# Attention over 1,601 keys in one core: the last key taken off, the half tile in two passes, other places for the side jobs

## The chip, the cores and the metric

One Trainium2 chip (trn2), one core of it. The metric is the device time of one execution in microseconds. Inputs lie in HBM, laid out beforehand on the host; the time covers one launch.

## The reference

`x` is 16 batches of 256 tokens of width 128, `ctx` 16 batches of 1,601 keys of width 96. All is float32.

```
def xattn(x, context, Wq, Wk, Wv, Wo, bo):        # 16 heads of 64
    q, k, v = (x @ Wq), (context @ Wk), (context @ Wv)
    attn = softmax(q k^T / 8)
    return (attn v) @ Wo + bo
x = x + xattn(layernorm(x), ctx, ...)
x = x + ffn(layernorm(x))     # 32 experts of 64, 4 of them per token by a grouped
                              # choice (2 of 4 groups), and one shared expert of 128
```

## The kernel before, in words

**Products.** Wq Wk^T and Wv Wo are multiplied head by head at the start (`A`, 128x96, and `B_all`, 96x128). A query is then a vector of width 96 that is multiplied with the raw keys, and the attention's output is a mean of raw keys, of width 96, that `B_all` projects. Every operand of a large matmul is split into a rounded part (`_hi`) and the rest (`_lo`), and a product takes three passes: hi x hi, hi x lo, lo x hi.

**Groups.** 16 batches x 4 groups of 4 heads are 64 groups. A group is 1,024 query columns (4 heads x 256 tokens) against 13 tiles of keys: 12 of 128, the last (s = 12) of 65 rows. The group's place in its batch is i (0 to 3).

**Per tile.** `scores(s)` (called qk here; L529, L532, L535) makes 128 x 1,024 scores in one half of the PSUM tile `st`: 3 passes x 2 matmuls of 512 columns. ScalarE takes the exponential twice, into `p_full` (L796) and rounded into `p_hi` (L799). VectorE (L1049; for tiles 3, 5, 7, 9 GpSimd, L410) makes `p_lo`. `weigh(s)` (called pv; L543, L546, L549) adds 3 passes x 2 matmuls to the output in PSUM, `op`, which ScalarE copies out once a group (`oT`, L771, `keep_output`).

**The order on TensorE** in a group is written out: for t = 2 to 12: qk(t), side jobs, pv(t-2), side jobs; then pv(11), scores(0) of the next group, pv(12), scores(1) of the next group. qk(2) of a group waits for the exponentials of its tile 0, pv(0) for the `oT` of the group before and for `p_lo` of tile 0.

**Side jobs** are small pieces of work for other groups, each with one letter. They use the two banks of the PSUM tile `side` in turn: job j waits until job j-2 is drained, that is read by VectorE (`s_drain`, which VectorE raises job by job, in order). `PLACES` and `EXTRA` say which jobs stand before and behind pv in each step t:

```
PLACES = {2: ("MM", "M"), 3: ("MM", "M"), 4: ("MM", "MM"), 5: ("MM", "M"), 6: ("MM", "MM"),
          7: ("MM", "MM"), 8: ("MM", "MY"), 9: ("MM", "MM"), 10: ("MM", "MM"), 11: ("YY", "YT"),
          12: ("", "QQ")}
EXTRA = {2: {5: "L", 6: "N"}, 3: {5: "R"}}
```

- M (32 a group, L475): plain scores of the next group for an upper bound of each query's maximum; VectorE reduces them (L1061), then `combine_max` (L920).
- T (L479): turns the maxima into a row; VectorE copies it (`m_row`, L925) and a DMA on SP's queue (L281) puts it under `qT_hi`, so that the scores come out with the maximum subtracted. scores(0) of the next group waits for it (`s_ml`).
- Y (4 a group, L555): `project_head`, the output of one head of the group before; on VectorE `add_head`: a reciprocal of the denominator (L930), a wait for it, two multiply-adds into `x1` (L933).
- Q (2 a group, L468 to L470): queries of the group after the next; ScalarE keeps hi (L734), VectorE lo (L916).
- L, N (L442), R: tokens of other batches turned, and the router's logits.

At the end of each group VectorE has small steps (`after_jobs`): i = 0 statistics, i = 1 normalisation and expert groups, i = 2 routing weights, i = 3 router scores. GpSimd also splits the next batch's keys, a quarter per group. At the start it splits the whole first batch (L365 to L369), and only then SP starts the loads of the second batch (`load_context`, L276, L277), and behind them the DMA of the first row of maxima.

The last 330 us are the experts (17 steps for each of 8 chunks of 512 tokens); the change leaves them as they are, but for the last group's Y jobs, which stand there.

Of the kernel before, what the change touches and what calls it, by code (L numbers as in the profile page):

```python
# [11 lines left out]
P = 128  # L12
# [6 lines left out]
def xattn_moe(nc, x, ctx_keys, ctx_turned, attn_w, bo, router_wT, router_b, moe_w, out):  # L19
# [6 lines left out]
    NC = 1601  # L26
# [14 lines left out]
    MAXW = KEYS // 4  # L41
    NM = 4 * (GQ // P)
    NCH = T // 4
    YW = D + 1
    OW = DC + 1

    stack = ExitStack()
    with stack:
# [24 lines left out]
        recip = sb(stack, "recip", [P, 2])  # L73
        spare = sb(stack, "spare", [P, 1])
# [38 lines left out]
        p_lo = sb(att, "p_lo", [P, 4, GQ], F32R)  # L113
# [4 lines left out]
        with ExitStack() as landing:  # L118
# [25 lines left out]
        s_set = sem("output_preset")  # L144
# [19 lines left out]
        s_drain = sem("side_job_used")  # L164
        s_sh = sem("context_piece_hi_kept")
# [4 lines left out]
        s_qk = sem("scores_made")  # L170
        s_ex = sem("probabilities_made")
# [89 lines left out]
        def _(sp):  # L261
# [7 lines left out]
            sp.dma_start(B_all[DC:OW, 0, 0:D], bo).then_inc(s_bo, 16)  # L269
# [932 lines left out]
```

## Time and profile before

| | |
|---|---|
| median of 3 runs | 3302.25 us (3302.05 to 3302.41) |
| the profiled execution's own time | 3302.1 us |
| its span, first to last instruction | 3300.3 us |
| TensorE busy | 3269.1 us (99%) |
| VectorE, ScalarE, GpSimd busy | 2383.1, 1938.2, 1069.6 us |
| chain that ended last | TensorE 98% |
| one group in the middle, from one qk(12) to the next | 1500.98 to 1546.41: 45.43 us |

In a timeline a row merges equal instructions in a row; its second figure is the time to the modelled end of the last of them. The first of each pair of matmuls overlaps the end of the one before, so what a piece of work costs TensorE is read as the distance from its start to the start of what follows it, not from its duration.

### The profile page before, as it was taken

What the parts mean: (1) busy time and instruction counts of PE and PEld (TensorE: products, weight loads), DVE (VectorE), ACT (ScalarE), POOL (GpSimd) and SP (SyncE); (2) the same over time, 40 slices, a digit from 0 to 9 for tenths busy, and PEclk for the clock granted to TensorE, in tenths of its full rate; (3) what the DMA queues carried; (4) which work ended last, traced back from release to release, by engine and by line L of the source; (5) the groups of instructions that cost most, each with busy time, mean ns of one, the idle gap of its engine ahead of it and who ended that gap; (6) DMA issues with size and microseconds to landing.
All of it is one profiled execution on the core that took longest, in us unless ns stands there. A gap on an engine that the chain in (4) does not pass through costs nothing.

```text
span 3300.3 us, 40940 instructions
## 1 busy us (share of the span) xinstructions
PE 3269.1 (99%) x15518; PEld 2606.8 (79%) x15518; DVE 2383.1 (72%) x4915; ACT 1938.2 (59%) x2236; POOL 1069.6 (32%) x710
## 2 busy tenths in 40 slices
PE   8999999999999999999999999999999999999999
PEld 6777777777787777877777777777777877777887
DVE  6777777777777777777777777777777777777655
ACT  4565555655556555665556655566655666575554
POOL 4322233222332233322233222322223322225555
PEclk9999999999999999999999999999999999999999
DMA  2000000000000000000000000000000001000000
GB/s 79 1 16 1 16 1 11 6 1 16 1 16 1 16 1 16 1 1 16 1 16 1 16 1 16 1 9 8 1 16 1 16 1 39 1 3 4 7 7 10
DMA packets 8055, 32.39 MB, mean 10 GB/s; under 512 B 1585, under 2 KB 2354, under 8 KB 7474
## 3 DMA queue, kind: packets, MB, share of 16 engines
q1 hardware_dynamic: 7858, 29.78, 2.9%
q8 instruction: 122, 2.00, 0.3%
q14 instruction: 75, 0.61, 0.1%
HBM read 27.41 MB, written 2.10 MB: 9 GB/s over the span
## 4 chain that ended last, share of the span: by engine, by line
PE 98%; DVE 1%; issue 0%; ACT 0%; DMA 0%; POOL 0%; POOLq 0%; DVEq 0%; ACTq 0%
PE st L529 12%; PE st L532 12%; PE st L535 12%; PE op L543 12%; PE op L549 12%; PE op L546 12%; PE side L475 11%; PE side L555 3%; PE st L636 2%; PE st L638 2%; PE st L637 2%; PE side L468 1%; PE side L470 1%; PE side L469 1%; PE op L636 1%; PE op L637 1%
## 5 line engine op out<-in xcount | busy, mean ns | idle before, releaser
L796 ACT ACTIVATE p_full<-st 128x1024 f32<-128x1024 f32 (+1 forms) x832 | 853.8, 1026 | 1128.5 <-PE st L535 1128.4
L1061 DVE TENSOR_REDUCE m_part<-side 128x1 f32<-128x402 f32 x2016 | 1078.2, 571 | 550.6 <-PE side L475 550.6
L410 POOL TENSOR_TENSOR p_lo<-p_full,p_hi 128x1024 fp32r<-128x1024 f32 x256 | 669.2, 2614 | 2063.7 <-ACT p_hi L799 2063.7
L799 ACT ACTIVATE p_hi<-st 128x1024 fp32r<-128x1024 f32 (+1 forms) x832 | 848.6, 1020 | 0.0
L1049 DVE TENSOR_TENSOR p_lo<-p_full,p_hi 128x1024 fp32r<-128x1024 f32 (+1 forms) x576 | 700.3, 1216 | 132.7 <-ACT p_hi L799 132.7
L475 PE MATMUL side<-cT_hi,qT_hi 96*128 96x402 f32 x2016 | 555.2, 346 | 0.0
L529 PE MATMUL st<-qT_hi,cT_hi 97*128 97x512 f32 (+1 forms) x1664 | 538.4, 405 | 2.3 <-DMA qT_hi<-m_row 2.3
L543 PE MATMUL op<-p_hi,v_hi 128*97 128x512 f32 (+1 forms) x1664 | 527.1, 398 | 0.5 <-DVE p_lo L1049 0.5
L532 PE MATMUL st<-qT_lo,cT_hi 96*128 96x512 f32 (+1 forms) x1664 | 524.8, 397 | 0.0
L535 PE MATMUL st<-qT_hi,cT_lo 96*128 96x512 f32 (+1 forms) x1664 | 521.9, 395 | 0.0
L549 PE MATMUL op<-p_hi,v_lo 128*97 128x512 f32 (+1 forms) x1664 | 521.1, 394 | 0.0
L546 PE MATMUL op<-p_lo,v_hi 128*97 128x512 f32 (+1 forms) x1664 | 520.8, 394 | 0.0
L475 PEld LDWEIGHTS side<-cT_hi,qT_hi 96*128 96x128 f32 x2016 | 379.6, 188 | 111.8
L532 PEld LDWEIGHTS st<-qT_lo,cT_hi 96*128 96x128 f32 (+1 forms) x1664 | 308.9, 186 | 79.8
L535 PEld LDWEIGHTS st<-qT_hi,cT_lo 96*128 96x128 f32 (+1 forms) x1664 | 306.8, 184 | 80.8
L549 PEld LDWEIGHTS op<-p_hi,v_lo 128*97 128x97 f32 (+1 forms) x1664 | 270.3, 162 | 115.4
L546 PEld LDWEIGHTS op<-p_lo,v_hi 128*97 128x97 f32 (+1 forms) x1664 | 270.1, 162 | 114.6
L529 PEld LDWEIGHTS st<-qT_hi,cT_hi 97*128 97x128 f32 (+1 forms) x1664 | 296.9, 186 | 32.4 <-issue 2.5
L543 PEld LDWEIGHTS op<-p_hi,v_hi 128*97 128x97 f32 (+1 forms) x1664 | 266.3, 164 | 31.7 <-DVE p_lo L1049 1.4
L427 POOL TENSOR_TENSOR h_lo<-hid,h_hi 128x512 fp32r<-128x512 f32 x136 | 175.9, 1293 | 152.0 <-ACT h_hi L840 151.9
L1128 DVE TENSOR_TENSOR gu_mul<-st,act_g 128x512 f32<-128x512 f32 x128 | 88.5, 691 | 106.6 <-PE side L694 99.0
L933 DVE SCALAR_TENSOR_TENSOR x<-side,recip,x 128x128 f32<-128x128 f32 x512 | 156.1, 347 | 9.0
(164 smaller groups left out, 2606.0 us busy)
## 6 DMA issues: line engine op xcount, KB each, us to landing
keys_nat<-in_ctx_keys SPq DMA_DIRECT2D x16, 624.0 KB, 5.8
keys_tur<-in_ctx_turned SPq DMA_DIRECT2D x16, 603.0 KB, 4.9
gud_raw<-in_moe_w SPq DMA_DIRECT2D x2, 1152.0 KB, 7.8
out_x<-x SPq DMA_DIRECT2D x8, 256.0 KB, 2.0
x<-in_x SPq DMA_DIRECT2D x1, 1920.0 KB, 12.1
qT_hi<-m_row SPq DMA_DIRECT2D x64, 4.0 KB
aw<-in_attn_w SPq DMA_DIRECT2D x2, 448.0 KB, 5.3
aw<-in_attn_w SPq DMA_DIRECT2D x1, 896.0 KB, 9.3
```

Of the source, the lines that this page charges most:

```text
L410: pool.tensor_tensor(p_lo[:, slot(s), :], p_full[:, s % 2, :], p_hi[:, slot(s), :].bitcast(F32), ALU.subtract).then_inc(s_lo_pool, 1)
L475: return pe.matmul(where[:, 0:MAXW], qT_hi[slot][0:DC, tile * P:(tile + 1) * P], cT_hi[par][0:DC, part * MAXW:(part + 1) * MAXW], start=Tr ...
L529: pe.matmul(st[0:m, s % 2, j, :], cT_hi[par][:, keys], qT_hi[slot][:, halves[j]], start=True, stop=False)
L532: pe.matmul(st[0:m, s % 2, j, :], cT_hi[par][0:DC, keys], qT_lo[slot][:, halves[j]], start=False, stop=False)
L535: mm = pe.matmul(st[0:m, s % 2, j, :], cT_lo[par][:, keys], qT_hi[slot][0:DC, halves[j]], start=False, stop=True)
L543: pe.matmul(op[0:OW, j, :], v_hi[par][0:m, s, :], p_hi[0:m, slot(s), halves[j]], start=(s == 0), stop=False)
L546: pe.matmul(op[0:OW, j, :], v_hi[par][0:m, s, :], p_lo[0:m, slot(s), halves[j]], start=False, stop=False)
L549: mm = pe.matmul(op[0:OW, j, :], v_lo[par][0:m, s, :], p_hi[0:m, slot(s), halves[j]], start=False, stop=(s == S - 1))
L796: act.activation(p_full[0:m, s % 2, :], both(st[0:m, s % 2]), ACT.Exp, scale=SCALE)
L799: act.activation(p_hi[0:m, slot(s), :], both(st[0:m, s % 2]), ACT.Exp, scale=SCALE).then_inc(s_ex, 1)
L1049: dve.tensor_tensor(p_lo[0:m, slot(s), :], p_full[0:m, s % 2, :], p_hi[0:m, slot(s), :].bitcast(F32), ALU.subtract).then_inc(s_lo, 1)
L1061: dve.tensor_reduce(m_part[:, at:at + 1], where[:, 0:MAXW], AX.X, ALU.max).then_inc(s_drain, 1)
```

## The change

- The key 1,600 is subtracted from all other keys of its batch (scores and weighted mean change by a constant): GpSimd does it in `shift`, for the first batch whole and for the others a quarter per group behind tile 3. The last key has then score 0 for every query; its exponential e^(-max) comes from `keep_last` on ScalarE (8 columns) and is added to the denominator in `add_head`, by one more VectorE instruction and wait. The key's own contribution to the output and the bias come back by one side job U per batch (i = 1, t = 5): a matmul of 128 columns and one addition on VectorE.
- The tile s = 12 has 64 keys. 128 rows of `cT_hi` hold 64 keys' hi and the same keys' lo, so qk(12) is 2 passes instead of 3; its two halves have to be added: ScalarE copies the lower 64 rows out of `st` (`low_half`), VectorE adds them (`sum_half`), and the exponentials read the sum. `p_hi` and `p_lo` lie one above the other in 128 rows, so pv(12) is 2 passes as well (`weigh_half`).
- M jobs have 400 columns instead of 402.
- Side jobs: QQ of t = 12 stands before pv(10), not behind it; N goes from t = 6 to t = 3.
- scores(1) of the next group stands before pv(12), not behind it; scores(0) waits for `sum_half` instead of for the exponentials.

The diff, cut to its core:

```diff
-                  12: ("", "QQ")}
-        EXTRA = {2: {5: "L", 6: "N"}, 3: {5: "R"}}
+                  12: ("QQ", "")}
+        EXTRA = {1: {5: "U"}, 2: {5: "L", 3: "N"}, 3: {5: "R"}}
...
+            def shift(cols, tiles):
+                n = tiles.stop - tiles.start
+                pool.tensor_scalar(keys_tur[:, cols], keys_tur[:, cols], keys_tur[:, NC:KEYS], None, ALU.subtract)
+                return pool.tensor_tensor(keys_nat[:, tiles, :], keys_nat[:, tiles, :],
+                                          keys_nat[:, S:S + 1, :].to_broadcast([P, n, DC]), ALU.subtract)
...
+            shift(slice(0, NC), slice(0, S)).then_inc(s_ss, 1)
+            pool.wait_ge(s_ss, 1)
+            pool.tensor_copy(v_hi[0][:, :, 0:DC], keys_nat[:, 0:S, :]).then_inc(s_sh, 1)
             pool.wait_ge(s_sh, 1)
+            split_lo(0, slice(0, NC), slice(0, S)).then_inc(s_v, NGB)
...
+            def taken_off(where, batch):
+                pe.matmul(where[:, 0:D], last_T[:, batch:batch + 1].to_broadcast([OW, P]), B_sum[:, :],
+                          start=True, stop=True).then_inc(s_fill, 1)
...
                 for j in range(2):
+                    mm = pe.matmul(st[:, s % 2, j, :], cT_hi[par][0:DC, keys], qT_lo[slot][:, halves[j]],
+                                   start=False, stop=(s == FULL))
+                for j in range(2 if s < FULL else 0):
+                    mm = pe.matmul(st[:, s % 2, j, :], cT_lo[par][:, keys], qT_hi[slot][0:DC, halves[j]],
+                                   start=False, stop=True)
...
-                pe.wait_ge(s_ex, n + S)
+                pe.wait_ge(s_sum, g + 1)
                 scores(0, (i + 1) % 2, next_par)
+                scores(1, (i + 1) % 2, next_par)
                 pv(S - 1)
-                scores(1, (i + 1) % 2, next_par)
...
+                low_half()
                 for k, j in enumerate(place["Q"]):
+                    queries_hi(bank(j), j + 1, k, i % 2)
+                exp(FULL)
+                if g < NG - 1:
+                    if g:
+                        act.wait_ge(s_drain, place["Y"][-1] + 1)
+                    keep_last(g + 1)
...
+            def add_head(where, filled, head, tiles):
+                group = head // GH
+                dve.wait_ge(s_el, group + 1)
                 dve.wait_ge(s_fill, filled)
                 ys = where[:, 0:2 * YW].rearrange("p (q y) -> p q y", q=2)
+                last = e_last[:, group % 2, head % GH * 2:head % GH * 2 + 2].rearrange("p (q y) -> p q y", q=2)
+                dve.tensor_tensor(whole[:, :].rearrange("p (q y) -> p q y", q=2), ys[:, :, D:YW], last,
+                                  ALU.add).then_inc(s_rc, 1)
+                dve.wait_ge(s_rc, 2 * head + 1)
+                dve.reciprocal(recip[:, :], whole[:, :]).then_inc(s_rc, 1)
+                dve.wait_ge(s_rc, 2 * head + 2)
...
+                def sum_half():
+                    dve.wait_ge(s_low, g + 1)
+                    dve.tensor_tensor(s_half[:, :], both(st[0:TAIL, FULL % 2]), s_half[:, :],
+                                      ALU.add).then_inc(s_sum, 1)
...
                 for t in range(2, S):
-                    side_jobs(at[t][0])
-                    lo(t - 1)
                     if t == S - 1:
+                        lo(t - 1)
+                        sum_half()
+                        side_jobs(at[t][0])
                         lo(t)
+                    else:
+                        side_jobs(at[t][0])
+                        lo(t - 1)
                     side_jobs(at[t][1])
```

On TensorE, from the last Y and T of step 11 (L555, L479) on, before: qk(12), pv(10), the first of the two Q jobs.

```order
L555 MATMUL side<-B_all,oT 128x129 [waits side_job_used]
L555 MATMUL side<-B_all,oT 128x129
L479 MATMUL side<-ident,m_neg 8x128 [waits maxima_combined,side_job_used]
L529 MATMUL st<-qT_hi,cT_hi 65x512 [waits probabilities_made]
L529 MATMUL st<-qT_hi,cT_hi 65x512
L532 MATMUL st<-qT_lo,cT_hi 65x512 x2
L535 MATMUL st<-qT_hi,cT_lo 65x512 x2
L543 MATMUL op<-p_hi,v_hi 97x512 [waits probabilities_lo_kept]
L543 MATMUL op<-p_hi,v_hi 97x512
L546 MATMUL op<-p_lo,v_hi 97x512 x2
L549 MATMUL op<-p_hi,v_lo 97x512 x2
L468 MATMUL side<-x_hi,A_hi 96x256 [waits side_job_used]
```

And the same place now (Y is L593, T is L503, qk(12) is L557 and L560, Q is L492 to L494):

```order
L593 MATMUL side<-B_all,oT 128x129 [waits side_job_used]
L593 MATMUL side<-B_all,oT 128x129
L503 MATMUL side<-ident,m_neg 8x128 [waits maxima_combined,side_job_used]
L557 MATMUL st<-qT_hi,cT_hi 128x512 [waits probabilities_made]
L557 MATMUL st<-qT_hi,cT_hi 128x512
L560 MATMUL st<-qT_lo,cT_hi 128x512 x2
L492 MATMUL side<-x_hi,A_hi 96x256 [waits side_job_used]
```

qk(12) has lost its third pass, and the Q jobs, whose first matmul waits for a drained bank, stand where pv(10) stood.

On VectorE, the same stretch before: the two Y jobs of step 11 (L930, L933), `p_lo` of tile 10 (L1049), the third Y, the copy of T (L925), `p_lo` of tile 11.

```order
L930 RECIPROCAL recip<-side 128x2 [waits side_job_made,side_job_used]
L933 SCALAR_TENSOR_TENSOR x<-side,recip,x 128x128 [waits denominators_inverted]
L933 SCALAR_TENSOR_TENSOR x<-side,recip,x 128x128
L1049 TENSOR_TENSOR p_lo<-p_full,p_hi 128x1024 [waits probabilities_made]
L930 RECIPROCAL recip<-side 128x2 [waits side_job_made,side_job_used]
L933 SCALAR_TENSOR_TENSOR x<-side,recip,x 128x128 [waits denominators_inverted]
L933 SCALAR_TENSOR_TENSOR x<-side,recip,x 128x128
L925 CAST m_row<-side 8x128 [waits side_job_made,maxima_row_landed]
L1049 TENSOR_TENSOR p_lo<-p_full,p_hi 128x1024 [waits probabilities_made]
```

And now, from the second Y of step 11 on:

```order
L999 TENSOR_TENSOR whole<-side,e_last 128x2 [waits side_job_made,last_key_exponentials_kept,side_job_used]
L1002 RECIPROCAL recip<-whole 128x2 [waits denominators_inverted]
L1005 SCALAR_TENSOR_TENSOR x<-side,recip,x 128x128 [waits denominators_inverted]
L1005 SCALAR_TENSOR_TENSOR x<-side,recip,x 128x128
L1119 TENSOR_TENSOR p_lo<-p_full,p_hi 128x1024 [waits probabilities_made]
L999 TENSOR_TENSOR whole<-side,e_last 128x2 [waits side_job_made,last_key_exponentials_kept,side_job_used]
L1002 RECIPROCAL recip<-whole 128x2 [waits denominators_inverted]
L1005 SCALAR_TENSOR_TENSOR x<-side,recip,x 128x128 [waits denominators_inverted]
L1005 SCALAR_TENSOR_TENSOR x<-side,recip,x 128x128
L991 CAST m_row<-side 8x128 [waits side_job_made,maxima_row_landed]
L1119 TENSOR_TENSOR p_lo<-p_full,p_hi 128x1024 [waits probabilities_made]
L1125 TENSOR_TENSOR s_half<-st,s_half 64x1024 [waits half_tile_low_scores_copied]
```

Each Y has one instruction and one wait more; the order of the Y jobs and of `p_lo` of tile 10 between them is as it was, and `sum_half` is new behind `p_lo` of tile 11.

## Rows read from the trace of the kernel before

**Rows 1.** Page: busy time of each engine.
```profile
PE 3269.1 (99%) x15518; PEld 2606.8 (79%) x15518; DVE 2383.1 (72%) x4915; ACT 1938.2 (59%) x2236; POOL 1069.6 (32%) x710
```

**Rows 2.** Waits of PE, longest in total: us, times, longest.
```profile
PE side L442 <- DVE m_part L1061: 7.7, 16, 0.5
```

**Rows 3.** Timeline of PE, end of a group: start, us, engine, line.
```profile
1500.50 0.61 PE L555 MATMUL side<-B_all,oT 97*128 97x129 f32 x4
1500.95 0.28 PE L479 MATMUL side<-ident,m_neg 128*8 128x128 f32 x1
1500.98 0.71 PE L529 MATMUL st<-qT_hi,cT_hi 97*65 97x512 f32 x2
1501.52 0.63 PE L532 MATMUL st<-qT_lo,cT_hi 96*65 96x512 f32 x2
...
1502.45 0.62 PE L543 MATMUL op<-p_hi,v_hi 128*97 128x512 f32 x2
...
1503.84 0.28 PE L468 MATMUL side<-x_hi,A_hi 128*96 128x256 f32 x1
...
1505.25 0.63 PE L543 MATMUL op<-p_hi,v_hi 128*97 128x512 f32 x2
...
1512.22 0.53 PE L475 MATMUL side<-cT_hi,qT_hi 96*128 96x402 f32 x2
1512.58 0.63 PE L543 MATMUL op<-p_hi,v_hi 128*97 128x512 f32 x2
```

**Rows 4.** Timeline of DVE, the same place.
```profile
1498.93 0.17 DVE L930 RECIPROCAL recip<-side 128x2 f32<-128x2 f32 x1 [0.81 <-PE side L555]
...
1499.78 0.17 DVE L930 RECIPROCAL recip<-side 128x2 f32<-128x2 f32 x1
...
1500.51 1.21 DVE L1049 TENSOR_TENSOR p_lo<-p_full,p_hi 128x1024 fp32r<-128x1024 f32 x1
1501.64 0.16 DVE L930 RECIPROCAL recip<-side 128x2 f32<-128x2 f32 x1
1501.84 0.61 DVE L933 SCALAR_TENSOR_TENSOR x<-side,recip,x 128x128 f32<-128x128 f32 x2
1502.37 0.27 DVE L925 CAST m_row<-side 8x128 fp32r<-8x128 f32 x1
```

**Rows 5.** Timeline of PE around an N job.
```profile
1618.71 0.53 PE L475 MATMUL side<-cT_hi,qT_hi 96*128 96x402 f32 x2
1619.73 0.44 PE L442 MATMUL side<-ident,xn 128*128 128x128 f32 x2 [0.48 <-DVE m_part L1061]
```

**Rows 6.** Timeline of PE, end of the last group: pv(12).
```profile
2965.69 0.70 PE L543 MATMUL op<-p_hi,v_hi 65*97 65x512 f32 x2 [0.49 <-DVE p_lo L1049]
2966.23 0.63 PE L546 MATMUL op<-p_lo,v_hi 65*97 65x512 f32 x2
```

**Rows 7.** Timeline of ACT: the two exponentials of tile 12.
```profile
1502.65 1.02 ACT L796 ACTIVATE p_full<-st 65x1024 f32<-65x1024 f32 x1 [2.29 <-PE st L535]
1503.57 1.01 ACT L799 ACTIVATE p_hi<-st 65x1024 fp32r<-65x1024 f32 x1
```

**Rows 8.** Timeline of DVE, first and last of the steps behind a group i = 1.
```profile
1597.91 1.10 DVE L900 TENSOR_SCALAR xn<-x,moments,rstd 128x128 f32<-128x128 f32 x4
...
1600.51 0.18 DVE L973 MAX8 best<-choice 128x8 f32<-128x32 f32 x1
```

**Rows 9.** Timeline of POOL, the split of the first batch.
```profile
22.90 1.23 POOL L365 CAST v_hi<-keys_nat 128x1248 fp32r<-128x1248 f32 x1
...
27.65 2.66 POOL L369 TENSOR_TENSOR v_lo<-keys_nat,v_hi 128x1248 fp32r<-128x1248 f32 x1
```

**Rows 10.** Timeline of PE, the first scores of the first group.
```profile
38.19 1.20 PE L529 MATMUL st<-qT_hi,cT_hi 97*128 97x512 f32 x2 [2.33 <-DMA qT_hi<-m_row]
```

**Rows 11.** Page: a DMA issue, KB each, us to landing.
```profile
keys_nat<-in_ctx_keys SPq DMA_DIRECT2D x16, 624.0 KB, 5.8
```

**Rows 12.** Windows: us, busy (count) of PE, PEld, DVE, ACT, POOL, PEclk, DMA share, GB/s.
```profile
40.00:42.00 2.00, 2.00 (x6) 1.58 (x5) 0.00 (x0) 0.71 (x1) 0.00 (x0) 0.50 0.00 0
1619.00:1622.00 3.00, 2.52 (x14) 1.93 (x12) 1.70 (x4) 0.89 (x3) 0.14 (x1) 1.00 0.00 0
```

More of the change, by code:

```diff
@@ L45, in xattn_moe @@
     OW = DC + 1
+    assert TAIL == P // 2 and NC % 4 == 0
     stack = ExitStack()
@@ L298, in body @@
                     load_moe_weights(2, 10, 16)
-                if last and i == NGB - 1:
+                if g == NG - 1:
                     sp.wait_ge(s_qk, (NG - 1) * S)
@@ L780, in x2_hi_of, with body @@
                                ACT.Copy).then_inc(s_xxh, 1)
-            def body(bb, par, i, last):
-                g = group_of(par, i)
-                n = (bb * (2 * NGB * S) + g * S)
-                first_bank = jobs_of(par, i, last)
-                jobs = (bb * (2 * PER_BATCH) + first_bank)
-                place = job_at(i, last)
+            def body(b, i, g):
+                n = g * S
+                place = jobs_at(g)
                 def exp(s):
                     m = rows(s)
-                    act.wait_ge(s_qk, n + (s + 1))
+                    if s < FULL:
+                        act.wait_ge(s_qk, n + (s + 1))
+                        made = both(st[:, s % 2])
+                    else:
+                        act.wait_ge(s_sum, g + 1)
+                        made = s_half[:, :]
@@ L1010, in _ @@
                 where = (st[:, 0], st[:, 1], op)[u % 3]
-                tile, part = u % (NM // 4), u // (NM // 4) * 2
+                tile, part = u % (NT), u // (NT) * 2
                 if u == NM // 2 - 2:
@@ L1015, in _ @@
                 dve.wait_ge(s_mx, u + 1)
-                dve.tensor_reduce(m_part[:, tile * 4 + part:tile * 4 + part + 2], where[:, :, 0:MAXW], AX.X,
+                dve.tensor_reduce(m_part[:, tile, part:part + 2], where[:, :, 0:MAXW], AX.X,
                                   ALU.max).then_inc(s_mxd, 1)
@@ L1031, in weights_lo, with body @@
                                   gud_hi[:, q, :, :].bitcast(F32), ALU.subtract).then_inc(s_wl, 1)
-            def body(bb, par, i, last):
-                if par == 0 and i == 0:
-                    steps[0] = head_steps
-                g = group_of(par, i)
-                n = (bb * (2 * NGB * S) + g * S)
-                first_bank = jobs_of(par, i, last)
-                jobs = (bb * (2 * PER_BATCH) + first_bank)
-                place = job_at(i, last)
-                links = (bb * links_per_turn)
+            def body(b, i, g):
+                n = g * S
+                place = jobs_at(g)
                 made = dict.fromkeys(KINDS, 0)
-                into = [(bb * 4 + (2 * par + (i + (NGB - 1)) // NGB * 2 + q)) for q in range(2)]
+                into = [2 * ((g - 1) // NGB) + 2 + q for q in range(2)]
                 def lo(s):
@@ L1102, in body @@
                     side_jobs(at[t][1])
-                    if last and i == NGB - 1:
+                    if g == NG - 1:
                         for q in (2 * t - 4, 2 * t - 3):
```

419 lines of the change are left out of this document (222 added, 197 removed).

## The prediction

> **What bounds the kernel now.** First the page's busy times [rows 1]: TensorE is busy 99% of the span, the next engine 72%. Then the waits of TensorE: the longest kind in the whole run is 7.7 us in 16 waits [rows 2]. So the attention runs at TensorE's own pace, and a matmul saved or a new wait of TensorE counts in full. Next the timeline of TensorE at the end of a group [rows 3]: two passes (four matmuls of 512 columns) go from 1501.52 to 1502.45, so one pass of two matmuls costs 0.465 us. The 65-row tile costs the same per pass as a full one. Last the timeline of VectorE at that place [rows 4], because the change moves a job there that waits for VectorE. I call the start of qk(12), 1500.98, time 0.
>
> **Passes removed.** One pass of qk(12) and one of pv(12) in each of 64 groups: 128 x 0.465 = 59.5 us off. Nothing else covers or needs that time.
>
> **Columns of M.** Two M jobs of 402 columns take 0.36 us [rows 3], 0.45 ns a column; 2,016 jobs x 2 columns are 1.8 us off.
>
> **N moved.** N stands third in a row behind MM and waits for the first of these reductions: it starts 1.02 us after the M pair [rows 5] instead of 0.37 us, 0.65 us lost. At t = 3 only one M stands ahead of it, and the job two before it has been drained during pv(1). 16 x 0.65 = 10.4 us off.
>
> **U added.** Four matmul instructions of a Y take 0.45 us [rows 3]; U has two, 0.225 us, and the change from a plain to a rounded product makes the next first pass 0.54 instead of 0.465 us [rows 3]. 16 x 0.30 = 4.8 us on. VectorE's addition for it stands in the middle of a group, where it has time.
>
> **Q moved.** This is the term that decides. Q0 waits until the job two before it, the last Y of step 11, is drained. Before, Q0 starts at +2.86 (1503.84), and that Y is drained at 1501.84 + 0.61 = 1502.45, +1.47: no wait. Now Q0 stands directly behind the shortened qk(12), which ends at 0.54 + 0.465 = +1.00. Even with the old `add_head` it would wait 0.5 us. And `add_head` grows by one small instruction and a wait for itself. That sum is in no row; from below it costs nothing, from above about as much as the reciprocal and its wait, 1501.84 - 1501.64 = 0.20 us. I take 0.21, since it is the same shape and also waits for its own end. VectorE works without a gap from the first Y of step 11 (which waits 0.81 us for TensorE, so it does not start earlier) to the last: 1498.93 is -2.05. First Y 0.85 + 0.21, second up to its last piece 0.20 + 0.21 + 0.53, so `p_lo` of tile 10 starts at -0.05 instead of 1500.51; it takes 1.13 (1500.51 to 1501.64); then 0.21 + 0.20 to the multiply-adds and 0.61 for them: drained at +2.10.
>
> From a VectorE end to the waiting start on TensorE the N row gives about 0.06 us (the first M's reduction). The wait of Q0 thus ends at 2.16. T is late too: it waits for the second Y, which now ends at +0.04, and starts at +0.10 instead of -0.03, which shifts qk(12) by 0.13. So per group T costs 0.13 and Q0 2.16 - 1.13 = 1.03 us. T 62 times: 8.1 us on; Q 61 times (groups 1 to 61 have both Y and Q): 62.8 us on. The nearest bounds of the Q wait are 0.53 (added sums free) and 1.1 us.
>
> After a wait the first pass is dearer as well: 0.54 us (2965.69 to 2966.23) instead of 0.465 [rows 6]; the weights were not in place. 61 x 0.07 = 4.3 us on. The Trainium skill (TensorE: Matmul & The Clock Gate, the table of specs, engine queue depth) says that TensorE can pull weight loads ahead of matmuls in flight; by that the 4.3 us would be hidden and the time 4.3 us lower. The row after a wait says otherwise, and I go by the row.
>
> **The half tile's chain.** qk(12) ends at 1.13; ScalarE starts 0.20 us behind a product (1502.45 to 1502.65) [rows 3, 7], copies the lower half from 1.33 to 2.35 (one exponential takes 1.02). VectorE: multiply-adds, T copy and `p_lo` of tile 11 end at 3.36; the sum, bounded by the 1.2 us of a `p_lo` of twice the rows, ends at 4.56. scores(0) now stands at: Q ends 2.16 + 1.41 = 3.57, with 0.07 on top, pv(10) and pv(11) 2.79 more, 6.4. No wait, 1.8 us to spare; the Q wait itself made that room. Then exponentials from 4.6 to 6.55 (0.92 + 1.01), `p_lo` of the half tile to 7.8; pv(12) stands at 9.2. No wait. The small steps behind the group take VectorE until 7.73 + 2.78 = 10.5 at worst (i = 1, 1597.91 to 1600.69) [rows 8]; `p_lo` of the next tile 0 then ends at 11.7 and pv(0) stands at 9.2 + 0.93 + 1.39 + 0.36 = 11.9. That is closed with 0.1 us to spare, and is what is late next. The output copy starts behind pv(12) at 10.3 and ends at 11.3, also in time; the exponentials of tile 1 end at 13.2 for a qk(3) at 13.4. GpSimd is busy 32% [rows 1]; `shift` stands between its tiles 3 and 5, with 4 us idle there. I cost these at nothing.
>
> **Start and end.** GpSimd must shift the first batch before it splits it: a pass over 1,600 elements, between 1.6 us (by the cast, 1.23 us for 1,248) and 3.4 us (by the subtraction, 2.66 us for 1,248), and one over 1,248 of 2.66 us [rows 9]. The split is complete 4.3 to 6.1 us later than 30.3. SP starts the second batch's loads only then, and the maxima's row behind them. A load lands 5.8 us after its issue [rows 11], so if the row waits behind them the first scores start 2.3 to 4.3 us later than 38.19 [rows 10]; if it doesn't, 0 to 1 us. I take 3.2 on. VectorE's sum over `B_all` (2,048 elements, about twice a `p_lo` row's 1.13 us) delays pv(0) behind group 0 once, 1 us on. In the last group nothing stands between qk(12) and pv(12) but pv(10) and pv(11), and pv(12) waited 0.49 us already [rows 6]; the chain copy, sum, exponentials makes it 3.3 us on. The last group's Y jobs among the experts: 0.5 on.
>
> **The sum.** -59.5 - 1.8 - 10.4 + 4.8 + 62.8 + 4.3 + 8.1 + 3.2 + 1 + 3.3 + 0.5 = +16.3 us. Against the profiled execution's 3302.1 us, which is the median (3302.25) within 0.2, this gives 3318.4 us: a little slower. A difference of 0.2%, 6.6 us, is about what a measurement of this kernel can tell from none.
>
> **Rivals.**
> - *Q waits less.* If the added sums in `add_head` cost VectorE nothing, Q0 waits 0.53 us and T not at all: 30.5 + 8.1 us less, 3280 us. For: they are 2 elements a row. Against: the reciprocal of the same shape takes 0.16 us and its wait 0.04. 7%.
> - *The change does what its list says* (the other side): TensorE keeps its pace and the removed passes count in full, from the point where the last Y is drained before qk(12) ends, which needs VectorE 1.2 us earlier. 3302.1 - 59.5 - 1.8 - 10.4 + 4.8 + 8.0 = 3243 us. For: TensorE hardly waited before. Against: rows 3 and 4, by which a Y is drained 0.47 us too late even unchanged. 5%.
> - *A second wait, at pv(0).* The half tile's chain on VectorE leaves 0.1 us at i = 1 and 0.4 at i = 2. If the sum from PSUM takes longer or the three engines' waits add up, pv(0) or qk(3) wait 0.5 us in 48 groups: 24 us more, 3342 us. 10%.
> - *The clock falls.* After the start's idle stretch (2.33 us before the first scores, and one transposition ahead of it) the granted clock is 0.50, 1.2 GHz, still at 40 to 42 us; in the stretch with the 0.65 us gap of N it is 1.00 [rows 10, 12]. If each Q wait brought back such a stretch of 4 us at half pace, it would cost 2 us x 61, 3440 us. The same page of the Trainium skill (Part 1) says that the clock is halved after an idle window and given back after a busy one; a wait of one microsecond between long busy stretches is nearer the N row. 3%.
>
> **How the numbers follow.** The forecast (both waits, as priced) has 70%, of which 6% fall within 0.2% because several terms are a few microseconds off; the rivals 7, 5, 10 and 3%; 5% are left for small sums near no change, 4 of them within 0.2%. Slower by over 0.2%: 64 + 10 + 3 + 1 = 78%. Within 0.2%: 6 + 4 = 10%. Faster: 7 + 5 = 12%. The range: from 3290, which takes the Q wait at 0.65 us, to 3337, most of the second wait; left out are the clock, the two faster rivals and a part of the third, together less than 20%. The forecast's own bounds are Q 0.9 to 1.1 us (-8, +4), the start (-3, +1).
>
> **What would show it.** In the changed profile: TensorE waits for VectorE's multiply-adds (L1005) at Q's first matmul (L492) about 61 times by near 1 us, and at T (L503) by 0.1; no waits at N (L466); pairs of `st` and `op` passes at 0.465 us as before; groups of 45.6 to 45.8 us instead of 45.4; first scores near 41 us; granted clock 1.00 between. Wrong is the forecast if L492 shows no wait or half of it (the first two rivals), if L570 or L557 wait for `p_lo` or `p_full` (the third), or if the clock row falls below 1.00 in the middle.

## The result and the profile after

| | before | changed |
|---|---|---|
| median | 3302.2 us (3302.05 to 3302.41) | 3326.62 us (3323.84 to 3327.17) |
| ratio | | 1.0072, interval 1.0055 to 1.009 |
| profiled execution, span | 3302.1, 3300.3 us | 3323.84, 3322.0 us |
| TensorE busy | 3269.1 us | 3231.1 us |
| VectorE, ScalarE, GpSimd busy | 2383.1, 1938.2, 1069.6 us | 2503.7, 2018.3, 1191.5 us |

The changed kernel is slower by 0.7%. TensorE has 38 us less to do and ends 21.7 us later: it now waits. A second set of runs of the unaltered changed kernel (

> The changed kernel once more, unaltered, for a second profile and its spread. Expected 3324 to 3327 us. Its groups should show the Q wait (L492 behind L1005) 61 times by 0.8 us idle; where its span differs from 3322.0 us, the place of the difference (start, a group kind, or the experts) tells what varies.

) gave 3326.41 us against 3300.38, ratio 1.0078 (1.0066 to 1.0091), with the same waits.

The page of the changed kernel, busy times, granted clock and chain, to be put beside [rows 1]:

```profile
PE 3231.1 (97%) x15278; PEld 2559.4 (77%) x15278; DVE 2503.7 (75%) x5240; ACT 2018.3 (61%) x2364; POOL 1191.5 (36%) x835
...
PEclk8999999999999999999999999999999999999999
...
PE 89%; DVE 6%; issue 3%; POOL 1%; ACT 0%; DMA 0%; DVEq 0%; POOLq 0%; SPq 0%; ACTq 0%
```

The clock is in the top tenth in every slice of 83 us after the first; one of them holds a short fall, which is told below. VectorE now has 6% of the chain that ended last. The waits of TensorE (us in total, times, longest), beside [rows 2]:

```profile
PE side L492 <- DVE x L1005: 50.7, 61, 0.8
PE st L557 <- DMA qT_hi<-m_row: 11.0, 1, 11.0
PE side L466 <- DVE xn L966: 6.2, 1, 6.2
...
PE op L570 <- DVE p_lo L1119: 3.5, 3, 2.5
```

The first matmul of the Q jobs (L492) waits 61 times for the last Y's multiply-adds (L1005); N (L466) waits no longer for a reduction. The end of a group on TensorE (start, us, engine, line), the place of [rows 3]:

```profile
1511.48 0.61 PE L593 MATMUL side<-B_all,oT 97*128 97x129 f32 x4
1512.04 0.27 PE L503 MATMUL side<-ident,m_neg 128*8 128x128 f32 x1
1512.07 0.71 PE L557 MATMUL st<-qT_hi,cT_hi 97*128 97x512 f32 x2
1512.62 0.63 PE L560 MATMUL st<-qT_lo,cT_hi 96*128 96x512 f32 x2
1514.09 0.36 PE L492 MATMUL side<-x_hi,A_hi 128*96 128x256 f32 x1 [0.84 <-DVE x L1005]
1514.29 0.28 PE L493 MATMUL side<-x_lo,A_hi 128*96 128x256 f32 x1
...
1518.36 0.63 PE L557 MATMUL st<-qT_hi,cT_hi 97*128 97x512 f32 x2
...
1522.08 0.63 PE L557 MATMUL st<-qT_hi,cT_hi 97*128 97x512 f32 x2
...
1523.83 0.40 PE L570 MATMUL op<-p_hi,v_hi 128*97 128x512 f32 x1
```

qk(12) now has two passes: the second starts at 1512.62 and leaves the engine at 1513.09 (0.47 later). Q0 starts at 1514.09: exactly 1.00 us lost. Its first pass takes 0.20 us (1514.09 to 1514.29), the later ones 0.12. From qk(12) to pv(0) of the next group it is 11.76 us; before it was 1500.98 to 1512.58, 11.60 us [rows 3]. So 0.93 us of passes came off and 1.09 us of waiting came on. VectorE at the same place, beside [rows 4]:

```profile
1510.98 0.16 DVE L999 TENSOR_TENSOR whole<-side,e_last 128x2 f32<-128x2 f32 x1
1511.17 0.17 DVE L1002 RECIPROCAL recip<-whole 128x2 f32<-128x2 f32 x1
1511.38 0.61 DVE L1005 SCALAR_TENSOR_TENSOR x<-side,recip,x 128x128 f32<-128x128 f32 x2
1511.90 1.22 DVE L1119 TENSOR_TENSOR p_lo<-p_full,p_hi 128x1024 fp32r<-128x1024 f32 x1
1513.03 0.15 DVE L999 TENSOR_TENSOR whole<-side,e_last 128x2 f32<-128x2 f32 x1
1513.22 0.17 DVE L1002 RECIPROCAL recip<-whole 128x2 f32<-128x2 f32 x1
1513.42 0.61 DVE L1005 SCALAR_TENSOR_TENSOR x<-side,recip,x 128x128 f32<-128x128 f32 x2
...
1515.28 1.21 DVE L1125 TENSOR_TENSOR s_half<-st,s_half 64x1024 f32<-64x1024 f32 x1
...
1518.56 1.22 DVE L1119 TENSOR_TENSOR p_hi<-p_full,p_hi 64x1024 fp32r<-64x1024 f32 x1 [0.88 <-ACT p_hi L851]
```

VectorE has no gap from the second Y to the last, and each Y costs it 0.19 to 0.20 us more (1510.98 to 1511.17: the added sum and the wait for it). The last Y is drained at 1514.03, and Q0 starts 0.06 us later.

Where the span's 21.7 us lie, by the times of T (L503, before L479), of the first scores and of the first expert matmul in both traces:

| stretch | changed less before | forecast |
|---|---|---|
| to the first scores (41.92 against 38.19) | +3.7 | +3.2 |
| first scores to T of group 0 | -1.7 | 0 |
| T of group 0 to T of group 62 (80.94 to 2939.47; before 78.93 to 2922.25) | +15.2 | +11.1 |
| T of group 62 to the experts (2988.46; before 2967.16) | +4.1 | +1.4 |
| experts | +0.4 | +0.5 |

### The profile page after: what moved, and what is told of

The parts are those of the page before. It is cut to its first block, busy times and chain, and to the rows that moved or that the text cites. A ratio compares the mean times of both kernels' runs of the same rounds, so it can differ in the third digit from the quotient of the medians.

```text
span 3322.0 us, 41110 instructions
## 1 busy us (share of the span) xinstructions
PE 3231.1 (97%) x15278; PEld 2559.4 (77%) x15278; DVE 2503.7 (75%) x5240; ACT 2018.3 (61%) x2364; POOL 1191.5 (36%) x835
## 4 chain that ended last, share of the span: by engine, by line
PE 89%; DVE 6%; issue 3%; POOL 1%; ACT 0%; DMA 0%; DVEq 0%; POOLq 0%; SPq 0%; ACTq 0%
PE side L499 11%; PE st L557 11%; PE st L560 11%; PE st L563 11%; PE op L570 10%; PE op L576 10%; PE op L573 10%; DVE x L1005 3%; PE side L593 2%; PE st L678 2%; PE st L680 2%; PE st L679 2%; PE side L492 1%; DVE recip L1002 1%; DVE whole L999 1%
## 5 line engine op out<-in xcount | busy, mean ns | idle before, releaser
L1136 DVE TENSOR_REDUCE m_part<-side 128x1 f32<-128x400 f32 x2016 | 1073.2, 569 | 480.2 <-PE side L499 480.0
L848 ACT ACTIVATE p_full<-st 128x1024 f32<-128x1024 f32 x768 | 788.6, 1027 | 885.7 <-PE st L563 880.6
L851 ACT ACTIVATE p_hi<-st 128x1024 fp32r<-128x1024 f32 x768 | 784.8, 1022 | 0.0
L1119 DVE TENSOR_TENSOR p_lo<-p_full,p_hi 128x1024 fp32r<-128x1024 f32 x512 | 622.5, 1216 | 46.0 <-ACT p_hi L851 45.2
L499 PE MATMUL side<-cT_hi,qT_hi 96*128 96x400 f32 x2016 | 555.0, 346 | 0.0
L557 PE MATMUL st<-qT_hi,cT_hi 97*128 97x512 f32 x1664 | 540.9, 406 | 11.8 <-DMA qT_hi<-m_row 11.0
L560 PE MATMUL st<-qT_lo,cT_hi 96*128 96x512 f32 x1664 | 524.7, 396 | 0.0
L570 PE MATMUL op<-p_hi,v_hi 128*97 128x512 f32 x1536 | 488.3, 399 | 3.7 <-DVE p_lo L1119 3.5
L573 PE MATMUL op<-p_lo,v_hi 128*97 128x512 f32 x1536 | 480.8, 394 | 0.0
L576 PE MATMUL op<-p_hi,v_lo 128*97 128x512 f32 x1536 | 480.6, 394 | 0.0
L560 PEld LDWEIGHTS st<-qT_lo,cT_hi 96*128 96x128 f32 x1664 | 315.3, 190 | 74.4
L557 PEld LDWEIGHTS st<-qT_hi,cT_hi 97*128 97x128 f32 x1664 | 295.4, 190 | 42.6 <-issue 11.2
```

The costliest lines, as they stand in the source:

```text
L499: return pe.matmul(where[:, 0:MAXW], qT_hi[slot][0:DC, tile * P:(tile + 1) * P], cT_hi[par][0:DC, part * MAXW:(part + 1) * MAXW], start=Tr ...
L557: pe.matmul(st[:, s % 2, j, :], cT_hi[par][:, keys], qT_hi[slot][:, halves[j]], start=True, stop=False)
L560: mm = pe.matmul(st[:, s % 2, j, :], cT_hi[par][0:DC, keys], qT_lo[slot][:, halves[j]], start=False, stop=(s == FULL))
L570: pe.matmul(op[0:OW, j, :], v_hi[par][:, s, :], p_hi[:, slot(s), halves[j]], start=(s == 0), stop=False)
L573: pe.matmul(op[0:OW, j, :], v_hi[par][:, s, :], p_lo[:, slot(s), halves[j]], start=False, stop=False)
L576: mm = pe.matmul(op[0:OW, j, :], v_lo[par][:, s, :], p_hi[:, slot(s), halves[j]], start=False, stop=False)
```

## The experiments

Each was measured beside the kernel before (medians 3300.4 to 3301.6 us), and each ratio below is against that. Differences in us are against `changed_again`, 3326.41 us, or, for the two variants of the kernel before, against its median of 3301.6 us.

**Is the Q jobs' place the cause?** `q_behind` puts them back behind pv(10) on TensorE. A second part of the edit, not shown, only keeps VectorE's order as it was.

```diff
-                  12: ("QQ", "")}
+                  12: ("", "QQ")}
```

> The changed kernel with the two Q jobs back behind pv(10) on TensorE; VectorE and ScalarE keep their order. Theory (the last Y is drained too late for Q0, and the group's end has no slack left): the 61 waits of L492 vanish, 66 us off; but pv(12), qk(2) and pv(0) come 1 us earlier and now meet the half tile's chain and the small steps on VectorE: pv(0) waits for p_lo about 1.1 us behind i = 1, 0.8 behind i = 2, 0.25 behind i = 3, none behind i = 0, 34 us, and about 0.1 us per group for p_lo of tile 10, 6 us. Expected 3300 us (3290 to 3310). Rival (the Q wait is the whole loss and nothing stands behind it): 3326 - 66 = 3260 us.

Measured: 3333.53 us (3332.29 to 3335.03), ratio 1.01 (1.0085 to 1.0116). A clear miss: the Q wait is gone, and the kernel is 7 us slower still, not 26 us faster. Its longest wait of TensorE:

```profile
PE st L557 <- ACT p_hi L851: 48.1, 63, 1.0
```

Its TensorE, the end of the same group:

```profile
1517.92 0.70 PE L557 MATMUL st<-qT_hi,cT_hi 97*128 97x512 f32 x2
1518.47 0.64 PE L560 MATMUL st<-qT_lo,cT_hi 96*128 96x512 f32 x2
...
1527.94 0.73 PE L557 MATMUL st<-qT_hi,cT_hi 97*128 97x512 f32 x2 [0.76 <-ACT p_hi L851]
```

And what came ahead of that on ScalarE (Q's copy, the first exponential of tile 12, both of the next tile 0) and on VectorE (the sum, `p_lo` of the half tile):

```profile
1521.41 1.30 ACT L776 ACTIVATE qT_hi<-side 96x512 fp32r<-96x512 f32 x2 [1.25 <-PE side L494]
1522.61 1.04 ACT L848 ACTIVATE p_full<-s_half 64x1024 f32<-64x1024 f32 x1
...
1525.95 1.03 ACT L848 ACTIVATE p_full<-st 128x1024 f32<-128x1024 f32 x1 [1.25 <-DVE p_hi L1119]
1526.88 1.01 ACT L851 ACTIVATE p_hi<-st 128x1024 fp32r<-128x1024 f32 x1
```

```profile
1521.13 1.21 DVE L1125 TENSOR_TENSOR s_half<-st,s_half 64x1024 f32<-64x1024 f32 x1
...
1524.64 1.22 DVE L1119 TENSOR_TENSOR p_hi<-p_full,p_hi 64x1024 fp32r<-64x1024 f32 x1 [1.11 <-ACT p_hi L851]
```

From qk(12) to qk(2) it is 10.02 us here and 10.01 in the changed kernel (1512.07 to 1522.08), with 8.9 us of TensorE's work in it. What fills the rest here is a chain off TensorE: two exponentials of tile 12, `p_lo` of tile 12, the next group's two exponentials of its tile 0, then qk(2). The first of the last two exponentials waits for `p_lo` of tile 12 (the 1.25 us above), because tile 12 and the next tile 0 share a slot of `p_full`. In the changed kernel the same step had 0.1 us to spare: that `p_lo` ends at 1519.78 and scores(0) at 1519.92. So two chains of nearly equal length cross the end of a group, and the wait of Q was only where the first of them showed.

What starts the second chain is not the same in the two kernels. In the changed kernel the exponential of tile 12 follows the sum at once, 0.03 us behind its end (1515.28 + 1.21 = 1516.49), and the sum ends a stretch without a gap on VectorE that begins with the Y jobs:

```profile
1516.52 1.06 ACT L848 ACTIVATE p_full<-s_half 64x1024 f32<-64x1024 f32 x1
```

In `q_behind` the sum ends at 1522.34, but the exponential starts at 1522.61, 0.27 us later, right behind Q's copy, which stands ahead of it on ScalarE and waits for products that TensorE now makes behind pv(10). The medians over 61 groups are the same 0.03 and 0.27 us. So up to 0.24 us a group of this chain (an estimate: 15 us in all) comes from Q's copy and not from VectorE; the exponentials ahead of the copy were not tried.

The 7 us on top are of the size of the dearer first pass behind the wait at qk(2): from there to pv(0) it takes 1.87 us (1527.94 to 1529.81) instead of 1.75 (1522.08 to 1523.83), 61 x 0.12 = 7 us.

**How much of it is the added sum?** `no_added_sum` takes the addition and its wait out of `add_head`; its denominators lack the last key. The diff leaves out the line that adjusts the remaining wait.

```diff
-                dve.tensor_tensor(whole[:, :].rearrange("p (q y) -> p q y", q=2), ys[:, :, D:YW], last,
-                                  ALU.add).then_inc(s_rc, 1)
-                dve.wait_ge(s_rc, 2 * head + 1)
-                dve.reciprocal(recip[:, :], whole[:, :]).then_inc(s_rc, 1)
+                dve.reciprocal(recip[:, :].rearrange("p (q y) -> p q y", q=2), ys[:, :, D:YW]).then_inc(s_rc, 1)
```

> The changed kernel without the addition of the last key's exponential to the denominator in add_head (its small instruction and its wait for itself are left out, so the denominator lacks that one key). Theory: each Y is 0.20 us shorter on VectorE, three of them lie in the chain to Q0, T's wait goes too: Q0 waits about 0.4 us (idle 0.25) instead of 1.0, 61 x 0.6 + 62 x 0.11 = 43 us off: 3283 us. Rival (the added sums are free, the wait comes from Q's new place alone): 3326 us and L492 as before.

Measured: 3289.97 us (3288.04 to 3290.53), ratio 0.9967 (0.9954 to 0.9979): 36.4 us less than `changed_again`, 0.6 us in each of 61 groups, three times the 0.2 us of one sum, as three Y jobs stand ahead of Q0. Its wait at Q:

```profile
PE side L492 <- DVE x L1002: 23.3, 61, 0.4
```

27 us came off this wait, 7 us can be the wait of T (62 x 0.11), which was in the forecast too. The rest of the wait, 0.4 us, is the 0.5 us that the prediction gave for the old `add_head`.

**Do the Y jobs' places matter?** `y_spread` moves two of the three Y jobs of step 11 into steps 2 and 3, so that only one is left ahead of T.

```diff
-        PLACES = {2: ("MM", "M"), 3: ("MM", "M"), 4: ("MM", "MM"), 5: ("MM", "M"), 6: ("MM", "MM"),
-                  7: ("MM", "MM"), 8: ("MM", "MY"), 9: ("MM", "MM"), 10: ("MM", "MM"), 11: ("YY", "YT"),
+        PLACES = {2: ("MM", "MY"), 3: ("MM", "MY"), 4: ("MM", "MM"), 5: ("MM", "M"), 6: ("MM", "MM"),
+                  7: ("MM", "MM"), 8: ("MM", "MY"), 9: ("MM", "MM"), 10: ("MM", "MM"), 11: ("Y", "T"),
```

> The changed kernel with two of the three Y jobs of step 11 moved to steps 2 and 3 (PLACES 2: MM, MY; 3: MM, MY; 11: Y, T); nothing is left out. New theory (the end of a group is one chain over VectorE and ScalarE: Y, Y, p_lo of tile 10, Y, copy of T, p_lo of tile 11, sum_half, two exponentials, p_lo of the half tile, two exponentials of the next tile 0, qk(2); from the start of qk(12) to that of qk(2) it takes 10.0 us wherever Q stands, against 8.9 of work on TensorE): without two Ys it is 1.9 us shorter, below TensorE's work, so the waits of L492 and L557 vanish and the distance falls to 9.0 us: 61 x 1.1 + T's 7 = 74 us off, some 5 us on for an N now third in a row: 3257 us (3250 to 3270). First rival (the reading of the prediction, small steps on VectorE ahead of pv(0) are next): 0.5 us stay at pv(0), 3290 us.

Measured: 3292.75 us (3290.52 to 3293.64), ratio 0.9977 (0.9967 to 0.9986). Direction right, size half: 33.7 us off. Both waits at the end of the group are gone, and qk(12) to qk(2) takes 8.92 us, all of it work:

```profile
1498.64 0.71 PE L557 MATMUL st<-qT_hi,cT_hi 97*128 97x512 f32 x2
...
1499.66 0.28 PE L492 MATMUL side<-x_hi,A_hi 128*96 128x256 f32 x1
...
1507.56 0.67 PE L557 MATMUL st<-qT_hi,cT_hi 97*128 97x512 f32 x2
```

But some of the time went into new waits, in the step to which the Y jobs went:

```profile
PE side L499 <- DVE x L1005: 13.7, 44, 0.4
...
PE side L466 <- DVE m_part L1136: 4.7, 16, 0.3
```

That is 18 us of the missing 32 or so (66 for the waits at the group's end, 61 x 1.09, less 33.7). The other 14 us may be dearer first passes: the mean of L557 is 412 ns instead of 406 over 1,664 matmuls, 10 us. But the next run argues against taking that for the whole.

**The same in the kernel before.** `before_y_spread` makes the same edit of `PLACES` in the kernel before, where nothing waits at the end of a group.

> The kernel before, with the Y jobs spread as in y_spread and nothing else. In the kernel before the group's end has slack, so spreading can only cost: each Y that stands alone makes one more first pass behind a plain product dearer by 0.08 us (two more per group, 10 us), and the second M of step 3 waits for a Y that VectorE drains late, behind p_lo of tile 1 (about 0.3 us in 44 to 62 groups with a dearer pass behind it, 15 to 20 us): 3325 to 3330 us beside 3300. That would be the part of the gain that y_spread did not show. If spreading costs nothing, it is 3300 us, and the missing 35 us of y_spread lie in the half tile itself.

Measured: 3306.91 us (3303.51 to 3308.12), ratio 1.0014 (1.0006 to 1.0023): 5.3 us, not the 25 to 30 that I had expected. No new wait of TensorE appears in its list. Spreading by itself costs little; the waits behind a Y need the longer `add_head` and the fuller VectorE (387 us busy in the 500 us from 1000 to 1500, before 368). How much of `y_spread`'s shortfall are dearer passes stays open, between 5 and 14 us.

**Q ahead in the kernel before.** `before_q_ahead` moves only the Q jobs ahead of pv(10) in the kernel before, behind its full qk(12).

```diff
-                  12: ("", "QQ")}
+                  12: ("QQ", "")}
```

> The kernel before with only the Q jobs moved ahead of pv(10) (VectorE keeps the order of its p_lo). There qk(12) ends 1.47 us behind its start and the last Y is drained at 1.47: Q0 waits 0.06 us and its first pass is up to 0.08 dearer; everything behind has slack. Expected 3300 to 3309 us beside 3300, so the new place is nearly free as long as qk(12) has three passes and add_head is short. If the new place is dear by itself (the reading that the job's place and not the chain's length counts): 3360 us.

Measured: 3308.55 us (3305.53 to 3309.92), ratio 1.0021 (1.0013 to 1.003), 7 us, near the upper end. There is no wait at Q long enough for its list. In its timeline the last pass of qk(12) starts at 1502.20, Q0 at 1502.72 and Q0's second pass at 1502.92: 0.52 us instead of 0.465, and 0.20 instead of 0.12. These 0.13 us are what was expected, and they are the 7 us: from T to T a group is 0.12 us longer than before, 7.3 us in 62 groups. So the move of Q alone makes next to no wait; it takes the shortened qk(12) and the longer `add_head` for one of 1 us.

**The start.** `row_first` has SP send the first row of maxima ahead of the second batch's loads.

```diff
-            load_context(1, NGB)
             send_max_row(J0_T + 1, 0)
+            load_context(1, NGB)
```

> The changed kernel with the DMA of the first row of maxima issued before the loads of the second batch. Theory (the row waits behind 1.27 MB of loads that themselves wait for the longer split on GpSimd): the row lands at about 33.3 us, the first scores start when the split is done, near 35.6 instead of 41.9: 6 us off, 3320 us. Rival (the first scores wait for the split, not for the row): 3326 us, first scores at 41 to 42.

Measured: 3319.9 us (3317.13 to 3323.16), ratio 1.0059 (1.0046 to 1.0072), 6.5 us less. In the changed kernel SP issues, in this order:

```profile
35.54 0.33 SPq L289 DMA_DIRECT2D keys_tur<-in_ctx_turned  x1
35.91 0.43 SPq L290 DMA_DIRECT2D keys_nat<-in_ctx_keys  x1
36.38 0.73 SPq L294 DMA_DIRECT2D qT_hi<-m_row  x1
```

and the first scores start at 41.92, 5.5 us behind the row's issue. In `row_first` the row is issued at 31.32 and the first scores wait for the split alone. (In `y_spread_row_first` the row is issued only at 36.61, and the first scores start at 38.60; executions start in more than one way, see the next section.)

```profile
35.56 1.22 PE L557 MATMUL st<-qT_hi,cT_hi 97*128 97x512 f32 x2 [4.58 <-POOL v_lo L392]
```

**The two together.** `y_spread_row_first`:

> The run y_spread with the first row of maxima sent before the second batch's loads: 6 us less than y_spread, as in row_first: 3251 us (3244 to 3264). If the two gains shared a cause, it would be equal to y_spread.

Measured: 3286.94 us (3284.8 to 3287.68), ratio 0.9958 (0.9944 to 0.9971). The start's 5.8 us add up with the rest.

**The two smaller moves.** `n_back` puts N back to t = 6.

```diff
-        EXTRA = {1: {5: "U"}, 2: {5: "L", 3: "N"}, 3: {5: "R"}}
+        EXTRA = {1: {5: "U"}, 2: {5: "L", 6: "N"}, 3: {5: "R"}}
```

> The changed kernel with the N job back at step 6, third in a row. Both theories: 16 waits of 0.65 us return, 10 us on, 3337 us. If the wait is swallowed by slack elsewhere: 3326 us.

Measured: 3338.03 us (3335.45 to 3338.22), ratio 1.0113 (1.0099 to 1.0127), 11.6 us more; the old wait is back with the same numbers as in [rows 2]:

```profile
PE side L466 <- DVE m_part L1136: 7.7, 16, 0.5
```

`half_tile_first` puts pv(12) back ahead of scores(1).

```diff
-                scores(1, (i + 1) % 2, next_par)
                 pv(S - 1)
+                scores(1, (i + 1) % 2, next_par)
```

> The changed kernel with pv(12) back ahead of scores(1) of the next group. pv(12) then stands when p_lo of the half tile ends (7.7 us behind qk(12)'s start for both). New theory: the chain to qk(2) runs over VectorE and ScalarE and does not pass through scores(1) or pv(12); pv(12) gets a wait of 0.1 us and a dearer first pass (0.07), which qk(2) inherits: 0 to 10 us on, 3326 to 3336. Rival (the order of pv(12) and scores(1) hides a wait of 1.4 us): 3326 + 62 x 1 = 3388 us.

Measured: 3330.8 us (3329.79 to 3331.54), ratio 1.0093 (1.0079 to 1.0107), 4.4 us more. So this part of the change is worth a few microseconds. In its trace pv(12) then starts 0.54 us behind the pass ahead of it (1521.77 to 1522.31) instead of 0.465, and its own first pass takes 0.54 (to 1522.85): the short wait and the dearer pass that were expected.

**A version that avoids most of the new waits.** `y_later_row_first` sends the row first and puts the Y jobs into steps 3 and 4, one M of step 4 into step 2.

```diff
-        PLACES = {2: ("MM", "M"), 3: ("MM", "M"), 4: ("MM", "MM"), 5: ("MM", "M"), 6: ("MM", "MM"),
-                  7: ("MM", "MM"), 8: ("MM", "MY"), 9: ("MM", "MM"), 10: ("MM", "MM"), 11: ("YY", "YT"),
+        PLACES = {2: ("MM", "MM"), 3: ("MM", "MY"), 4: ("MM", "MY"), 5: ("MM", "M"), 6: ("MM", "MM"),
+                  7: ("MM", "MM"), 8: ("MM", "MY"), 9: ("MM", "MM"), 10: ("MM", "MM"), 11: ("Y", "T"),
```

> y_spread_row_first with the first Y at step 4 instead of step 2 and one M at step 2 for it (PLACES 2: MM, MM; 3: MM, MY; 4: MM, MY). Steps 4 and 5 have no or one p_lo on VectorE, so the waits of M behind Y (14 us in 44 waits) should go: 3287 - 15 = 3272 us. If only their place changes: 3287 us.

Measured: 3274.6 us (3272.09 to 3276.2), ratio 0.992 (0.9907 to 0.9934), faster than both kernels. It is 12.3 us below `y_spread_row_first`, and no M waits for a Y any more. One wait has grown: N, now behind more jobs of step 3, waits 8.9 us in 16 times for the reduction ahead of it (4.7 us in `y_spread`), so this is not the end of it. Windows of 500 us (us, busy and count of PE, PEld, DVE, ACT, POOL, then PEclk, DMA share, GB/s), first of the changed kernel, then of this one; before, TensorE was busy 498.55 us of the same stretch.

```profile
1000.00:1500.00 500.00, 490.87 (x2342) 388.77 (x2341) 387.13 (x829) 312.06 (x348) 166.38 (x114) 1.00 0.02 6
```

```profile
1000.00:1500.00 500.00, 497.78 (x2381) 393.95 (x2380) 395.19 (x845) 315.22 (x352) 170.71 (x117) 1.00 0.03 9
```

TensorE's idle time falls from 9.1 to 2.2 us in 500. Over the 2,859 us of the 62 groups that is 39 us, most of the 45.3 us between `row_first` and this one.

## Why the prediction was right, and where it was wrong

The forecast of 3318.4 us was 8.2 us below the median and 5.4 us below the profiled execution, with the right sign, inside the range. By its steps:

- **Q moved: right.** 61 waits; 1.00 us lost in each (1513.09 to 1514.09), I had 1.03. VectorE's stretch without a gap and the 0.2 us of an added sum came as worked out. T is late by 0.11 us (1511.93 to 1512.04), I had 0.13.
- **The first pass after a wait: right.** 0.20 instead of 0.12 us at Q0, 0.08 x 61 = 4.9 us against 4.3 forecast. I had set beside it the Trainium skill (TensorE: Matmul & The Clock Gate, the table of specs, engine queue depth), by which TensorE pulls weight loads ahead of matmuls in flight. The traces agree with it where matmuls follow each other: before, the load for the Q0 of 1503.84 starts 0.23 us ahead of it (first line). They show no such lead across a wait: the load for the Q0 that waits starts with it (second line).

```profile
1503.61 0.16 PEld L468 LDWEIGHTS side<-x_hi,A_hi 128*96 128x96 f32 x1
```

```profile
1514.09 0.16 PEld L492 LDWEIGHTS side<-x_hi,A_hi 128*96 128x96 f32 x1 [1.27 <-DVE x L1005]
```

- **N, and the passes: right.** `n_back` says 11.6 us, I had 10.4. The removed passes went off in full at 0.465 us: 11.60 - 0.93 + 1.00 + 0.08 is 11.75, and 11.76 was measured.
- **The clock: right for Q, but not everywhere.** The granted clock is 1.00 in every window of 400 to 500 us from 100 to 3000 us, and in those of 2 us around the wait shown above (1512 to 1522), so the waits of 0.84 us between long busy stretches did not bring it down. It fell once, in group 1: pv(0) there waits 2.49 us for VectorE's sum over `B_all`. The granted clock is 0.75 from 94 to 96 us, 0.50 (1.2 GHz) from 96 to 98 and 1.00 again from 100 us; a pass takes 0.85 us (95.59 to 96.44) instead of 0.465. That was in no term. The length of a wait alone does not tell: at the last group's end TensorE waits 0.40 and 2.81 us within 5 us, and the clock is 1.00 in every window of 2 us there.

```profile
95.59 1.05 PE L576 MATMUL op<-p_hi,v_lo 128*97 128x512 f32 x2
```

```profile
96.00:98.00 2.00, 2.00 (x6) 1.65 (x5) 0.88 (x2) 0.24 (x1) 0.00 (x0) 0.50 0.00 0
```

- **The half tile's chain: wrong.** This is the step that failed, though it cost the sum little. I found "no wait, 1.8 us to spare" at scores(0) and named pv(0) as late next. The chain is closed one step earlier: exp(0) of the next group waits for `p_lo` of tile 12, because they share a slot of `p_full`, and had 0.1 us to spare (1519.78 against 1519.92), and qk(2) waits for that. I had compared each consumer's time with its own producer only and left out the slot. So I expected 3300 us of `q_behind` and got 3333.5. Q's copy on ScalarE ahead of the half tile's exponentials was missing from that expectation as well.
- **The wait at pv(0), the third rival: there, but small.** I had left 0.1 us to spare behind groups i = 1. There is none: behind each of them `p_lo` of tile 0 ends too late (the lines are VectorE's, then TensorE's), and pv(0) starts 1.91 us behind qk(2) (1613.83) instead of 1.75. `half_tile_first` bears it out: it makes the other groups 0.11 us longer and these 0.00. In 16 groups this is some 2.5 us, not 24.

```profile
1614.37 1.23 DVE L1119 TENSOR_TENSOR p_lo<-p_full,p_hi 128x1024 fp32r<-128x1024 f32 x1
```

```profile
1615.74 0.67 PE L570 MATMUL op<-p_hi,v_hi 128*97 128x512 f32 x2
```

- **Start: right by luck.** +3.7 against 3.2 in these two profiled executions, and the row waited behind the loads, as assumed. But GpSimd's `shift` of 1,600 elements took 4.33 us, outside my 1.6 to 3.4, and the two executions do not start alike. With the same code at the start, GpSimd begins the `shift` at 20.7 us here and at 22.8 to 22.9 in `q_behind`, `n_back`, `y_spread` and `no_added_sum`, and the first scores stand at 41.92 here and at 44.10 to 44.23 there. The kernel before has its first GpSimd piece at 22.90 [rows 9], as in those four; beside them the start costs 5.9 to 6.0 us, beyond my bound of 4.3. What decides how an execution starts was not looked for.
- **The sum over `B_all`: too small.** It takes VectorE 3.90 us, I had twice 1.13. With the fallen clock behind it, group 1 (T of group 0 to T of group 1) is 3.7 us longer than before, where my terms give 0.5.
- **Terms that I left out.** Group 0 no longer has the four Y jobs (it has no group before it): -1.8 us. And group 62, which has no Q jobs, shows the second chain bare. TensorE of the changed kernel:

```profile
2942.83 0.70 PE L570 MATMUL op<-p_hi,v_hi 128*97 128x512 f32 x2 [0.60 <-DVE p_lo L1119]
...
2949.29 0.73 PE L557 MATMUL st<-qT_hi,cT_hi 97*128 97x512 f32 x2 [0.86 <-ACT p_hi L851]
...
2987.45 0.70 PE L584 MATMUL op<-p_hi,v_hi 128*97 128x512 f32 x2 [2.81 <-DVE p_hi L1119]
```

The first two are the end of group 62, some 2.6 us that were in no term; the last is pv(12) of the last group. From the last qk(12) to the first expert matmul it is 8.8 us (2979.66 to 2988.46) instead of 6.4 (2960.77 to 2967.16): 2.4 us more, which is the forecast's 3.3 less the 0.93 of removed passes. Had I asked what the groups without Q do, I should have met the second chain before the run.

**What is left.** Between T of group 0 and T of group 62 the measured 15.2 us are 4.1 above the forecast: 3.2 from group 1 and 2.5 from pv(0) behind i = 1, less about 3 us, as the waits of Q and T were a little shorter than forecast and the move of N was worth a little more; some 1.4 us stay open. The median lies 2.8 us above the profiled execution. The unaltered repeat has the same spread (3323.93 to 3327.12), and its profiled execution, 3323.93, has the early start as well, while those of the four late starts lie in the upper part of their runs. So the two starts, 2.2 us apart, are the likely reason; no trace of a slower run of this kernel shows it.

## What to carry to other kernels

When an engine with 99% busy time loses work at one place, list for that place every chain that the other engines run across it, with the slots that tie them (here `p_full` by two tiles) and the order on each engine (here Q's copy ahead of an exponential), and take the longest: a chain that was covered by the removed passes becomes the bound, and moving the one job that shows the wait uncovers the next. What helps is to move work out of the stretch that all these chains share, here two `project_head` jobs, and to look where it lands: one step later was worth 12 us. A small DMA whose landing starts the whole pipeline belongs ahead of bulk loads on its queue.

## What the runs showed of the hardware

GpSimd at the start of the changed kernel:

```profile
20.70 4.33 POOL L381 TENSOR_SCALAR keys_tur<-keys_tur 96x1600 f32<-96x1600 f32 x1
...
29.24 3.42 POOL L387 TENSOR_TENSOR cT_lo<-keys_tur,cT_hi 96x1536 fp32r<-96x1536 f32 x1
```

A subtraction of one value per partition (2.7 ns an element) was slower here than one of two full operands (2.2 ns). I had expected it between a cast and a subtraction. The second thing is in the section above: a TensorE pass behind a wait cost 0.08 us more at 256 columns, and a stop ahead of qk(2) 0.12 us more up to pv(0), so here a wait cost more than the idle time that the list of waits shows.
